# First layer's attention of a two-layer transformer: ScalarE empties the denominators' and outputs' banks, and the reciprocal is taken on 8 rows

## What is computed

```python
sim = jnp.einsum('bhid,bhjd->bhij', q, k) * ATTN_SCALE          # + bias, causal mask
attn = jax.nn.softmax(sim, axis=-1)
out = jnp.einsum('bhij,bhjd->bhid', attn, v)
out = out.transpose(0, 2, 1, 3).reshape(b, n, HEADS * DIM_HEAD)
return out @ w_out
```

## Time and profile before

| | us |
|---|---|
| median of 3 runs | 2222.0 (2215.68 to 2233.71) |
| the profiled execution, its own time | 2209.62 |
| its span, first to last instruction | 2207.8 |
| the attention's slots within the span | about 252 to 1373 |

### The profile page before, as it was taken

One profiled execution on the slowest core, in us unless ns is written; L12 is line 12 of the kernel. 1 busy time (PEld: TensorE's weight loads), 2 busy tenths in 40 slices (PEclk: granted clock), 3 DMA queues, 4 the chain that ended last, 5 costly groups with the idle time before them and its releaser, 6 DMA issues. The chain is left out here.

```text
span 2207.8 us, 33163 instructions
## 1 busy us (share of the span) xinstructions
PE 1829.6 (83%) x11995; PEld 794.4 (36%) x11995; DVE 1294.9 (59%) x2140; ACT 884.0 (40%) x1393; POOL 749.8 (34%) x423
## 2 busy tenths in 40 slices
PE   1876889988889888898988886437989999899998
PEld 1455342433433334334343332225642233233233
DVE  6334765666666656667666542761156666766663
ACT  0213244444444444444444343022325455554555
POOL 1504636446355462553734565360007000000000
PEclk9898689989899898998998998659997889988898
DMA  4132100000000000000000000133321000000000
GB/s 144 53 109 56 24 5 1 7 5 6 6 1 8 5 7 2 5 8 5 1 7 1 1 1 22 39 120 87 92 68 34 25 25 15 13 25 25 25 1 20
DMA packets 52523, 61.01 MB, mean 28 GB/s; under 512 B 11386, under 2 KB 40334, under 8 KB 51470
## 3 DMA queue, kind: packets, MB, share of 16 engines
q1 hardware_dynamic: 48270, 50.52, 7.4%
q0 software_dynamic: 4096, 8.40, 1.4%
HBM read 35.09 MB, written 19.40 MB: 25 GB/s over the span
## 5 line engine op out<-in xcount | busy, mean ns | idle before, releaser
L1329 POOL TENSOR_TENSOR a_prob_sum<-a_prob_sum,a_prob 128x1024 f32<-128x1024 f32 (+2 forms) x224 | 479.6, 2141 | 260.7 <-ACT a_prob L1280 243.8
L1280 ACT ACTIVATE a_prob<-a_st,a_table 128x512 f32<-128x512 f32 (+3 forms) x640 | 367.4, 620 | 405.8 <-PE a_st L1173 245.3
L1375 DVE TENSOR_REDUCE a_maxima<-a_ring 128x16 f32<-128x512 f32 (+3 forms) x640 | 358.2, 604 | 292.3 <-PE a_ring L1104 148.8
L1766 DVE TENSOR_REDUCE a_maxima<-a_mx 128x1 f32<-128x512 f32 (+3 forms) x640 | 354.4, 605 | 166.8 <-PE a_mx L1753 125.7
L2024 ACT ACTIVATE a_prob<-a_st 128x1024 f32<-128x1024 f32 (+1 forms) x320 | 274.6, 900 | 247.0 <-PE a_st L1923 126.8
L1202 PE MATMUL a_ot<-a_prob,a_values 128*64 128x512 f32 (+3 forms) x1280 | 322.4, 584 | 60.4 <-DVE a_out_t L1444 60.4
L1753 PE MATMUL a_mx<-a_ks,a_qs 49*128 49x512 bf16 (+3 forms) x640 | 176.4, 390 | 32.2 <-DVE a_maxima L1766 29.5
L1104 PE MATMUL a_ring<-a_k_hi,a_q_hi 64*128 64x512 f16 (+3 forms) x640 | 147.8, 375 | 60.4 <-DVE a_maxima L1375 34.3
L1940 PE MATMUL a_ot<-a_prob,a_values 128*32 128x512 f32 (+3 forms) x1280 | 183.1, 628 | 0.0
L1325 POOL TENSOR_TENSOR a_prob_sum<-a_prob 128x1024 f32<-128x1024 f32 (+1 forms) x32 | 72.3, 2259 | 250.1 <-ACT a_prob L1280 118.7
L1390 DVE RECIPROCAL a_rden<-a_ring 128x512 f32<-128x512 f32 x32 | 107.4, 3356 | 53.2 <-PE a_ring L1147 52.0
(11 more groups left out here) (245 smaller groups left out, 2384.4 us busy)
## 6 DMA issues: line engine op xcount, KB each, us to landing
f_w<-in_w SPq DMA_DIRECT2D x28, 256.0 KB, 2.9
expert_in<-zeros SPq DMA_DIRECT2D x5, 1024.0 KB, 10.8
f_rows<-expert_in SPq DMA_DIRECT2D x16, 256.0 KB, 3.6
a_values<-values_all SPq DMA_DIRECT2D x8, 512.0 KB
expert_out<-f_result SPq DMA_DIRECT2D x16, 256.0 KB, 2.5
shared_w<-in_w SPq DMA_DIRECT2D x12, 256.0 KB, 2.9
parts<-p_part_t SPq DMA_DIRECT2D x6, 512.0 KB, 2.7
a_table<-in_head_table SPq DMA_DIRECT2D x16, 140.5 KB, 2.1
```

The source lines that it names most:

```text
L1280: e = act.activation(prob[:, s % NPROB, a, c0:QW], ps_st[s % 2][:, a, c0:QW], ACT.Exp, bias=table[x][:, a, at:at + 1])
L1329: pool.tensor_tensor(into[:, :, c0:QW], into[:, :, c0:QW], here[:, :, c0:QW], ALU.add).then_inc(added, 2 if r == TPQ - 2 else 1)
L1375: dve.reduce_max(maxima[:, qt // TPQ, a, qt % TPQ, at:at + count], bank[:, 0:hi - lo].rearrange("p (w k) -> p w k", k=WINDOW), AX_X).then_ ...
L1766: dve.reduce_max(own.maxima[:, qt // TPQ, a, qt % TPQ, n:n + 1], bank[:, 0:hi - lo], AX_X).then_inc(done, 1)
```

## The change

ScalarE, not VectorE, reads both banks. The denominators are copied from the ring into `den` at slot e+2, and the raw outputs from `ps_ot` into `out_raw` (two buffers) at slot e+3, which is what TensorE now waits for (`ot_read`). SyncE turns the two rows of `den` that matter (partitions 0 and 64, 512 each) into 8 rows of 128 with two transfers; VectorE takes the reciprocal of those 8x128 at slot e+4; SyncE stores them to a tensor in DRAM, waits, and at slot e+5 reads them back spread over 64 partitions per head with two transfers. VectorE multiplies `out_raw` by `rden` at slot e+6, both now in SBUF, and the unit `out` moves to slot e+7. The last pair gets 7 closing slots, not 4, and the load of the next `w_out` moves from slot 3 to slot 7. The `den` unit counts as one that ScalarE reads.

```diff
-SCALE_AT0 = {(end + 3) % NS0: qb for qb, end in enumerate(ENDS0)}
-OUT_AT0 = {(end + 4) % NS0: qb for qb, end in enumerate(ENDS0)}
+TAKE_AT0 = {(end + 3) % NS0: qb for qb, end in enumerate(ENDS0)}
+INVERT_AT0 = {(end + 4) % NS0: qb for qb, end in enumerate(ENDS0)}
+SPREAD_AT0 = {(end + 5) % NS0: qb for qb, end in enumerate(ENDS0)}
+SCALE_AT0 = {(end + 6) % NS0: qb for qb, end in enumerate(ENDS0)}
+OUT_AT0 = {(end + 7) % NS0: qb for qb, end in enumerate(ENDS0)}
+TAIL0 = 7
...
-            one.append(ring.put("den", (x, DEN_AT0[s])))
+            one.append(ring.put("den", (x, DEN_AT0[s]), True))
...
+            def turn_den():
+                for a in range(2):
+                    sp.dma_start(den_rows[TPQ * a:TPQ * a + TPQ, :],
+                                 den[64 * a:64 * a + 1, :].rearrange("o (t p) -> o t p", p=P)).then_inc(den_turned, 16)
+
+            def store_inverse(count):
+                sp.wait_ge(inverted, count + 1)
+                sp.dma_start(rden_wide.rearrange("a (t p) -> (a t) p", p=P), rden_rows[:, :]).then_inc(rden_stored, 16)
+
+            def spread_inverse(count):
+                sp.wait_ge(rden_stored, 16 * count + 16)
+                for a in range(2):
+                    sp.dma_start(rden[64 * a:64 * a + 64, :],
+                                 rden_wide[a:a + 1, :].to_broadcast([64, QW])).then_inc(rden_loaded, 16)
...
-                    if s == 3 and more:
+                    if s == TAIL0 and more:
...
-                    pe.wait_ge(ot_read, i * (2 * NQB) + outs_before(x, qb) + 1)
+                    pe.wait_ge(scaled, i * (2 * NQB) + outs_before(x, qb) + 1)
...
+            def take_out(qb, slots, count):
+
+                act.wait_ge(pv_done, slots)
+                if is_past(count - 1):
+                    act.wait_ge(scaled, count - 1)
+                act.activation(out_raw[qb % 2][:, :], ps_ot[:, :], ACT.Copy).then_inc(ot_read, 1)
...
+                elif kind == "den":
+                    if is_past(count):
+                        act.wait_ge(den_turned, 32 * count)
+                    act.activation(den[:, :], bank[:, :], ACT.Copy).then_inc(done_a, 1)
...
-                elif kind == "den":
-                    dve.reciprocal(rden[:, :], bank[:, :]).then_inc(done_v, 1)
...
-                dve.wait_ge(pv_done, slots)
-                dve.wait_ge(done_v, den_done)
-                dve.tensor_tensor(out_t[:, :], ps_ot[:, :], rden[:, :], ALU.mult).then_inc(ot_read, 1)
+            def invert(count):
+                dve.wait_ge(den_turned, 32 * count + 32)
+                dve.reciprocal(rden_rows[:, :], den_rows[:, :]).then_inc(inverted, 1)
+
+            def scale_out(qb, count):
+
+                dve.wait_ge(rden_loaded, 32 * count + 32)
+                dve.wait_ge(ot_read, count + 1)
+                dve.tensor_tensor(out_t[:, :], out_raw[qb % 2][:, :], rden[:, :], ALU.mult).then_inc(scaled, 1)
```

More of the change, by code:

```diff
@@ L865, in prologue0, with is_born @@
     return out, ring
+def is_born(x, qb, first):
+    return not (first and x == 0) if qb == NQB - 1 else x < 2
 def slots0(first, last):
@@ L871, in slots0 @@
     out = []
-    for n in range(2 * NS0 + (4 if last else 0)):
+    for n in range(2 * NS0 + (TAIL0 if last else 0)):
         x, s = divmod(n, NS0)
@@ L886, in slots0 @@
                 one.append(ring.put("turn", (x + ahead, qb)))
-        unborn = first and x == 0 and s < 4
-        if s in DEN_AT0 and unborn:
+        if s in DEN_AT0 and not is_born(x, DEN_AT0[s], first):
             ring.skip()
         elif s in DEN_AT0:
-            one.append(ring.put("den", (x, DEN_AT0[s])))
+            one.append(ring.put("den", (x, DEN_AT0[s]), True))
         if more and s < QK_UNITS0:
@@ L897, in slots0 @@
             two += [ring.put("trans", (x + 1, k, TRANS_AT0[s])) for k in range(2)]
-        if s in OUT_AT0 and unborn:
+        if s in OUT_AT0 and not is_born(x, OUT_AT0[s], first):
             ring.skip()
@@ L966, in attention0 @@
         ones = sb("ones", [P, DH0])
+        den = sb("den", [P, QW])
+        den_rows = sb("den_rows", [2 * TPQ, P])
+        rden_rows = sb("rden_rows", [2 * TPQ, P])
+        rden_wide = nc.dram_tensor("rden_wide", (2, QW), F32).ap()
         rden = sb("rden", [P, QW])
+        out_raw = [sb(f"out_raw{k}", [P, QW]) for k in range(2)]
         out_t = sb("out_t", [P, QW])
@@ L994, in attention0 @@
         ot_read = sem("ot_read")
+        den_turned = sem("den_turned")
+        inverted = sem("inverted")
+        rden_stored = sem("rden_stored")
+        rden_loaded = sem("rden_loaded")
+        scaled = sem("scaled")
         cleared = sem("cleared")
@@ L1006, in bank_of, with is_past @@
             return ring[unit.at % RING0]
+        def is_past(count):
+            return not (isinstance(count, int) and count <= 0)
         def outs_before(x, qb):
@@ L1041, in step @@
                         load_pair(1 - x, 2 * i + x + 1)
+                    if s in INVERT_AT0 and is_born(x, INVERT_AT0[s], first):
+                        store_inverse(i * (2 * NQB) + outs_before(x, INVERT_AT0[s]))
+                    if s in SPREAD_AT0 and is_born(x, SPREAD_AT0[s], first):
+                        spread_inverse(i * (2 * NQB) + outs_before(x, SPREAD_AT0[s]))
                     for unit in one + two:
@@ L1045, in step @@
                             turn_row(unit.what[0] % 2, unit.what[1])
+                        if unit.kind == "den":
+                            sp.wait_ge(done_a, base_a + unit.nth + 1)
+                            turn_den()
                         if unit.kind == "v" and unit.what[1] == 0:
@@ L1239, in _, with take @@
         def _(act):
-            def take(unit, base):
+            def take_out(qb, slots, count):
[3 more added lines that the diff above has]
+                act.activation(out_raw[qb % 2][:, :], ps_ot[:, :], ACT.Copy).then_inc(ot_read, 1)
+            def take(unit, base, count=0):
                 kind, what, bank = unit.kind, unit.what, bank_of(unit)
@@ L1270, in step @@
                     more = x == 0 or (x == 1 and not last)
+                    if s in TAKE_AT0 and is_born(x, TAKE_AT0[s], first):
+                        take_out(TAKE_AT0[s], slots - 2, i * (2 * NQB) + outs_before(x, TAKE_AT0[s]))
                     if x < 2:
@@ L1286, in step @@
                     for unit in one + two:
-                        if unit.acts or unit.kind == "trans":
+                        if unit.kind == "den":
+                            take(unit, base, i * (2 * NQB) + outs_before(*unit.what))
+                        elif unit.acts or unit.kind == "trans":
                             take(unit, base)
@@ L1438, in normalise @@
                 dve.tensor_tensor(rows, rows, r.unsqueeze(3).to_broadcast([P, TPQ, 4, DH0]), ALU.mult).then_inc(qn_done, 1)
-            def scale_out(i, x, qb, slots, den_done):
-                dve.wait_ge(pv_done, slots)
-                dve.wait_ge(done_v, den_done)
-                dve.tensor_tensor(out_t[:, :], ps_ot[:, :], rden[:, :], ALU.mult).then_inc(ot_read, 1)
+            def invert(count):
[5 more added lines that the diff above has]
+                dve.tensor_tensor(out_t[:, :], out_raw[qb % 2][:, :], rden[:, :], ALU.mult).then_inc(scaled, 1)
             def step(i, first=False, last=False):
                 base = base0(i)
-                dens = {}
                 for n, x, s, one, two in slots0(first, last)[0]:
@@ L1451, in step @@
                     more = x == 0 or (x == 1 and not last)
[L1452 to L1457, removed]
+                    if s in INVERT_AT0 and is_born(x, INVERT_AT0[s], first):
+                        invert(i * (2 * NQB) + outs_before(x, INVERT_AT0[s]))
+                    if s in SCALE_AT0 and is_born(x, SCALE_AT0[s], first):
+                        scale_out(SCALE_AT0[s], i * (2 * NQB) + outs_before(x, SCALE_AT0[s]))
                     for unit in one:
```

## The result

The changed kernel takes 2114.1 us (median of 4 runs, 2099.3 to 2119.5) against 2218.8 for the kernel before (2200.9 to 2233.7): 0.952 of its time, 95% interval 0.943 to 0.961. That is 105 us less, where 51 were forecast. It lies 6 us under the range given for 8 in 10 chances (2120 to 2206) and 31 us under the forecast's own (2145 to 2199). A second set of runs of the same kernel, beside three of the experiments, gave 0.955 (0.950 to 0.960), as expected of it.

A forecast was written before the change was run, and what follows sets the result against it. TensorE, busy 975 of 1121 us in the attention's stretch, was taken as the bound. Terms -84 - 30 + 8 + 17 + 13 + 9 + 10 + 6 = -51 gave 2171 us from 2222; own range 2145 to 2199, 8 in 10 2120 to 2206.

The forecast's parts named there:

- waits of the division: TensorE's waits for VectorE's product out of `ps_ot` (60.4 us) and its reciprocal (23.5) go: 83.9 us less.
- clock: Low clock at slots 2 and 14 goes, -30 us; `out` work may fall into it; new stalls at slots 10 and 29, +10.
- chain of transfers, uncovered: Small transfers and reciprocal before VectorE's slot e+6: wait of 0 to 1 us there, charged 1 us a pair, +8 us.
- product against GpSimd at slot 29: Product with two SBUF inputs waits for GpSimd's add at slot 29: +2.4 us in 7 pairs, 17 us.
- out ahead of the scores at slot 10: Block 0's `out` in slot 10 stands ahead of slot 11's scores, whose 0.9 us are no longer hidden; lower end 6 us.
- arrears in slots 13 to 16: TensorE runs into VectorE's arrears, its wait at slot 16 nearly doubles: +1.3 us in 7 pairs, 9 us (0 to 14).
- the end: Last block: copy, transfers and short reciprocal take 10.2 us, against reciprocal 3.36 and 0.46 to the product before: +6 us.
- C: Rival: late chain holds VectorE at slots e+4 and e+6, TensorE stands on the ring; at 3 us +45, 2267; chance 0.07.
- rival A: Nearly everything comes back, collisions hide and no new low stretch appears: -100 us, 2122; chance 0.14.
- A's sign: TensorE's idle time falling under 50 us would show that rival A is right.

The follow-up runs named there:

- the wide reciprocal: The change without its small transfers, VectorE inverting the whole 128x512 copy in SBUF at slot e+4: 2156.6 us, ratio 0.980 to the kernel before.
- two more trips: The change with the store of the inverted rows made three times, each waited for: 2173.3 us, ratio 0.988 to the kernel before.
- the second run: The unaltered change, measured again beside three of the experiments: ratio 0.955 (0.950 to 0.960) to the kernel before.

## Why the prediction was wrong, step by step

The direction and the place of the gain were right; the size wasn't. The forecast's terms against the profiles, us (the "rest" is slots 1, 17, 22, 30 and 39 with -0.2, the 3.9 that the account leaves, and -3.8 outside the attention):

```
term                                      forecast   measured
waits of the division                       -84       -83.5
clock (-30, +7 at out, +10 new)             -13       -22.9
chain of transfers, uncovered                +8        +2.3
product against GpSimd at slot 29           +17        +3.0
out ahead of the scores at slot 10           +6        +6.1
arrears in slots 13 to 16                    +9        +3.2
the end                                      +6        +4.5
rest of the slots, other stages               0        -7.8
sum                                         -51       -95.1
```

- **The waits of the division** went as worked out, 83.5 of 83.9 us, and the low clock at slots 2 and 14 went with them. That step is right, as is the 0.9 us for the reciprocal and the hidden copies (0.60 us each, and 0.4 us of waits for them).
- **The step that failed most is the price of slot 29, 17 us where 3.0 came, "Added: the product now has two SBUF inputs".** The rule was right: a product takes 0.68 us alone and up to 2.86 beside an add. Wrong was that L1402's collision was kept and a second put behind it. In the change L1459, the same operation, takes 0.44 us in all 7 pairs, where it took 2.29. The traces put it down to the move of `out`. Where `out` stands in slot 27 it delays slot 28's scores by 1 us, so GpSimd has a gap and begins its next add 0.36 us ahead of VectorE. With `out` in slot 30 or 31 the adds follow each other, and VectorE comes first as one ends; GpSimd's four adds then take 10.31 us. The other kernels agree: 2.28 to 2.29 us with the short reciprocal and with the outputs' copy alone, both with `out` in slot 27; 0.44 us with `out` in 30 or 31 in all five other kernels that have the change's copies, rows of 128 and full additions. Two kernels with `out` in slot 30 lie between, 1.87 us with the wide reciprocal and 1.21 with half the additions, since each moves one of the two engines again. No run moved `out` alone from slot 27: in every kernel where it left, the product had left slot 26 too. So this cause is argued from the times of the traces, not tested. One collision took the place of the other, +3.0 us and not +17.
- **The chain** is 5.8 us, not 6.6: the store's next step follows 1.22 us after its issue (740.78 to 742.00), where I had taken 2.4 from a load, while the spread took 3.57, not 3.0. The 0.1 us for each of four steps stands in no row; the one that the trace shows took 0.03 (740.75 to 740.78). By their own terms the chain's two ends would be 5.3 us and, since the spread's two transfers run side by side, 8.2 us, not 5.5 and 9; neither entered the sum. Outside slot 29 a late product reaches TensorE once, in the last pair, where it comes 1.7 us late and then meets an add: TensorE stands 2.33 us at slot 6.

```profile
1185.33 2.86 DVE L1505 TENSOR_TENSOR a_out_t<-a_out_raw,a_rden 128x512 f32<-128x512 f32 x1 [1.71 <-DMA a_rden<-rden_wide]
```

The forecast's reason, that a late product is covered by the ring, holds only up to here: 1.25 us more cost 20 us, 2.5 us more some 74. C had set its point of decision at 1.6 us of wait a block. With two more trips VectorE waits 88.1/32 = 2.8 us, and the kernel is still 1.2% faster than before, because outside slot 29 most of those waits stay hidden.

- **The clock** gave back 22.9 us net, where I had taken 13. The same kernel with the same idle time (67.6 and 67.4 us) had 91.3 us of low clock in one execution and 69.6 in the other, so this term is known to some 10 us only. Slot 29's new low stretches came as feared, 20 us of low clock at slots 29 and 30 together, but only 7 in the second run.
- **The arrears** of slots 13 to 16 came to a third of what was set, **the end** to three quarters.

So the mechanism of the gain was right, and the sizes were off to one side: the product, the chain and `out` were taken at or near their upper ends, the arrears and the new low clock in the middle, and only `out` came so. The sum of rival A, -100 us with a chance of 0.14, is the one nearest to what came, but partly by luck. A new low stretch did appear, idle time is 67.6 us and not under the 50 that was to be A's sign, and the 12 us that slots 29, 10 and 13 to 16 added, which A left out, are made up for by the smaller chain and by a rest of 7.8 us that no one had in the sum.

## What to carry to other kernels

When an operation on a shared engine is long, ask first what its length alone is worth: here a reciprocal 2.4 us shorter gave four fifths of the gain, while taking one bank away from the long one gave 18 us and taking both away, with later places, 43. A moved operation shifts the phase of the engines around it, so a collision seen in the trace of before must be worked out again with the new times, not carried over. And try work that may be late behind the work that feeds the busiest engine, not ahead of it: this took 15 us off slot 29 in both kernels that had it, but only one of them, 17.6 us faster, can be told from the change.

## What the runs showed of the hardware

- VectorE took a reciprocal of fp32 in 3.36 us for 512 columns and 0.93 for 128, the same on 8 rows as on 128 (0.93 and 0.96): the cost goes by the columns, so fewer columns, on as many rows as that needs, is the form to look for.
- VectorE and GpSimd lose more to each other than the forecast saw. Halving GpSimd's additions, which end hardly any of TensorE's waits themselves, gave 54 us, and 36 in the kernel before. The Trainium skill's "SBUF — State Buffer", section "Who interferes with whom", has the rule behind it, and says too that the order of issue decides who blocks. The traces agree: the 128x272 operation of the `negate` took 2.29 us where GpSimd's add had begun 0.36 us earlier (793.05 and 793.41), and 0.44 us where the add began 0.09 us later (744.29 and 744.38).
- Small transfers took different times by kind, each from its first issue to the step behind it: 2.36 us for two from SBUF to SBUF (737.45 to 739.81), 1.22 for 4 KB to DRAM (740.78 to 742.00), and 3.57 for the two that spread a row of DRAM over 64 partitions each (742.00 to 745.57).
